# A language-model layer on one core: attention as straight code in place of a loop of four sequences, and the expert lists with one moving operand

## The chip, the cores and the metric

The kernel runs on one core of a Trainium2 chip. The metric is device time in microseconds (us) of one execution; lower is better. The core has TensorE (PE, with PEld its weight loads), VectorE (DVE), ScalarE (ACT), GpSimd (POOL) and SyncE (SP), each with an instruction stream of its own. They meet at semaphores.

## The reference

32 sequences of 512 tokens, width 256, float32:

```
h = (tok_table[x] + pos_table + seg_table[seg]) * sqrt(256)
h = h + attention(layernorm(h))
h = h + ffn(layernorm(h))
attention(x): Q, K, V = x@wq, x@wk, x@wv            # 16 heads of 16, window of 64 keys
              GQ = x@wgq; GK, GV = mean over 8 tokens of x@wgk, x@wgv   # 8 heads, 64 latents
              out = (sigmoid(gl) * local(Q,K,V) + sigmoid(gr) * (remote(GQ,GK,GV) @ r_out_w)) @ w_out
ffn(x): scores = layernorm(x) @ centroids.T          # 8 experts
        expert e takes the 2048 highest scoring tokens that no earlier expert took
        out = x + gelu(layernorm(x) @ w1[e] + b1[e]) @ w2[e] + b2[e], scattered back
```

## The kernel before

The program has two phases. In the **attention** phase the sequences pass through the five engines one by one, software-pipelined: `sequence(b, q)` exists once for each engine and walks through the same `plan` of ten half-steps (scores by query for the row maxima, scores by key, exponentials, values, projections for the next sequence, output of the one before). Every engine computes, at build time, the semaphore count that each of its waits needs, in the class `Misc` (line 409 is one of those waits, issued by PE before it reuses a PSUM bank) and, on VectorE, in `chain` (line 1135), which makes an instruction wait for the one before it.

Sequences 0 and 1 are written out. Sequences 2 to 29 are seven passes through a loop whose body is four sequences, on every engine. Sequences 30 and 31, and step 32, which drains the pipeline, are written out again. On PE:

```
sequence(0, 0)
sequence(1, 1)
with pe.Fori(0, (SEQS - 4) // HB) as i:
    for r in range(HB):
        sequence(HB * i + 2 + r, (2 + r) % HB)
for b in range(SEQS - 2, SEQS + 1):
    sequence(b, b % HB)
```

In the loop `b` is an expression of a register, so each wait whose count depends on `b` is preceded by arithmetic on the engine's sequencer, and addresses of the embedding indices, of the scores and of the stored rows are computed there too. In the written-out sequences they are constants. A sequence of PE begins with `top_scores` for the latents: masks (line 994, 16 matmuls) and then line 1009, 128 small matmuls of 32x64 by 32x64 in one run. Before it stand the waits for what the other engines have to give.

In the **expert** phase (a loop over 7 experts and the eighth written out) PE runs `pe_expert`: per group of 512 tokens the first layer (line 911) and the second (line 924). Between them it serves the choice of the next expert's tokens, `pe_choice` and `dve_choice`, in slots set by the tables `pe_at` and `dve_at`: a radix search for the threshold, then a list of the 2048 chosen tokens. For the list VectorE builds `ohA` (which of 16 columns a token goes to), `ohP` (that times the partition number) and `ohT` (that times 128 x the tile number), and eight pieces `ohB` (lines 1292 to 1302). PE multiplies each `ohB` tile by `ohP` and by `ohT` (line 857), 32 matmuls for a piece, all summed into the 16 columns `LPS`. VectorE copies them into `idx_next` (line 1307), by which GpSimd gathers the rows of the next expert. For expert 0 the same is done before the loop with nothing beside it.

Of the kernel before, what the change touches and what calls it, by code (L numbers as in the profile page):

```python
# [26 lines left out]
P = 128  # L27
# [63 lines left out]
def tower(nc, ins, out, cin, din, widths, SEQS, S, V, F, E):  # L91
# [12 lines left out]
    with ctx:  # L104
# [141 lines left out]

        hits = sb("hits", [P, RADIX - 1, NT], BF16)
        ohA = sb("ohA", [P, NT, CT], BF16)
        ohP = sb("ohP", [P, NT, CT], BF16)
        ohT = sb("ohT", [P, NT, CT], BF16)  # L250
        ohB = sb("ohB", [P, 2, LT, P], BF16)
        w1 = sb("w1", [P, KC, F])
        w2 = sb("w2", [P, FC, D])
# [180 lines left out]
        def _(sp):  # L434
# [43 lines left out]

            store(0, 0)
            store(1, 1)  # L480
            with sp.Fori(0, (SEQS - 4) // HB) as i:
                for r in range(HB):
                    store(HB * i + 2 + r, (2 + r) % HB)
            for b in range(SEQS - 2, SEQS + 1):
                store(b, b % HB)
            sp.wait_ge(s_h1out[0], 16 * (NT // 2 + 1))
            sp.wait_ge(s_h1out[1], 16 * (NT // 2 + 1))
# [99 lines left out]
        def _(pool):  # L587
# [21 lines left out]

            sequence(0, 0)  # L610
            sequence(1, 1)
            with pool.Fori(0, (SEQS - 4) // HB) as i:
                for r in range(HB):
                    sequence(HB * i + 2 + r, (2 + r) % HB)
            for b in range(SEQS - 2, SEQS + 1):
                sequence(b, b % HB)

            pool.wait_ge(s_h1out[0], 16 * (NT // 2 + 1))
# [114 lines left out]
        @block.scalar  # L733
        def _(act):

            act.wait_ge(s_init, 3)
            m = Misc("head")
            for task in head_tasks:
                act_misc(act, m, task, None, 0)

            def sequence(b, q):
                m = Misc(b, q % 2)
                nx = 1 - q % 2
                for s in range(NU):
                    for task in plan[2 * s]:
                        act_misc(act, m, task, b, nx)
                    first, rest = plan[2 * s + 1][0], plan[2 * s + 1][1:]
                    run = m.old if s == 0 else m.new
                    if run:
                        act_exp(act, NU * b + s - 1, (s - 1) % NU, 0)  # L750
                    act_misc(act, m, first, b, nx)
                    if run:
                        act_exp(act, NU * b + s - 1, (s - 1) % NU, 1)
                    for task in rest:
                        act_misc(act, m, task, b, nx)

            sequence(0, 0)
            sequence(1, 1)
            with act.Fori(0, (SEQS - 4) // HB) as i:
                for r in range(HB):  # L760
                    sequence(HB * i + 2 + r, (2 + r) % HB)
            for b in range(SEQS - 2, SEQS + 1):
                sequence(b, b % HB)

            nc.scalar.activation(scr[:, :], c_ident[:, 0:1], ACT.Copy).then_inc(s_hid, 2)
            act_group(act, 0, 0)
            with act.Fori(0, E - 1) as e:
                act_expert(act, e, False)
            act_expert(act, E - 1, True)
# [58 lines left out]
            mm.then_inc(s_misc, 1)  # L828


        LPS = M_ps[1][:, 0:CT]

        def pe_choice(pe, n, part, k):
            if part == "radix":
# [14 lines left out]
            elif part == "list":  # L849
# [2 lines left out]
                    pe.wait_ge(s_ohA, n + 1)  # L852
                pe.wait_ge(s_ohB, LC * n + k + 1)
                for j in range(LT):
                    for half in (ohP, ohT):
                        first_, last_ = k == 0 and j == 0 and half is ohP, k == LC - 1 and j == LT - 1 and half is ohT
                        mm = nc.tensor.matmul(LPS, ohB[:, k % 2, j, :], half[:, k * LT + j, :],
                                              start=first_, stop=last_)
                mm.then_inc(s_used, 1)


# [77 lines left out]
        def _(pe):  # L939
# [169 lines left out]

            sequence(0, 0)  # L1110
            sequence(1, 1)
            with pe.Fori(0, (SEQS - 4) // HB) as i:
                for r in range(HB):
                    sequence(HB * i + 2 + r, (2 + r) % HB)
            for b in range(SEQS - 2, SEQS + 1):
                sequence(b, b % HB)

            pe.wait_ge(s_mA, Misc(SEQS).end("A"))
# [120 lines left out]
        def dve_choice(dve, n, part, k, base):  # L1239
# [51 lines left out]
            elif part == "places":  # L1291
                chain(dve, nc.vector.tensor_tensor(ohA[:, :, :], rhigh[:, :].unsqueeze(2).to_broadcast([P, NT, CT]),
                                                   laneb[:, 0:CT].unsqueeze(1).to_broadcast([P, NT, CT]),
                                                   ALU.is_equal), base)
                nc.vector.tensor_scalar(ohP[:, :, :], ohA[:, :, :], c_part, None, ALU.mult)
                nc.vector.scalar_tensor_tensor(out=ohT[:, :, :], in0=ohA[:, :, :], scalar=float(P),
                                               in1=laneb[:, 0:NT].unsqueeze(2).to_broadcast([P, NT, CT]),
                                               op0=ALU.mult, op1=ALU.mult).then_inc(s_ohA, 1)
            elif part == "list":
# [4 lines left out]
                                        ALU.is_equal).then_inc(s_ohB, 1)  # L1304
            elif part == "numbers":
                dve.wait_ge(s_used, LC * n + LC)
                nc.vector.tensor_copy(idx_next[:, :], LPS).then_inc(s_next, 1)

        def dve_prefix(dve, base):

# [61 lines left out]
        def _(dve):  # L1372
# [96 lines left out]
                    for task in half:  # L1469
                        dve_misc(dve, m, task, b, q, base)  # L1470

            sequence(0, 0, 0)
            PER = CH["n"]
            sequence(1, 1, 0)
            PER = CH["n"] - PER
            base = CH["n"]
            CH["n"] = 0
            with dve.Fori(0, (SEQS - 4) // HB) as i:
                for r in range(HB):
                    sequence(HB * i + 2 + r, (2 + r) % HB, HB * PER * i + base)  # L1480
            assert CH["n"] == HB * PER, CH["n"]
            base += PER * (SEQS - 4)
            CH["n"] = 0
            for b in range(SEQS - 2, SEQS + 1):
                sequence(b, b % HB, base)

            for t in range(TS):
                dve.wait_ge(s_rows[t], 16 * (SEQS + 1))
# [13 lines left out]
            dve_scales(dve, 0, base)  # L1502
            base += CH["n"]
            CH["n"] = 0
            PER2 = 6 * DIGITS + 2 * GR + 23
            with dve.Fori(0, E - 1) as e:
                dve_expert(dve, e, False, PER2 * e + base)
            assert CH["n"] == PER2, CH["n"]
# [32 lines left out]
```

## Time and profile before

| | |
|---|---|
| median of 3 runs | 3180.93 us (3177.55 to 3189.85) |
| the profiled execution's own time | 3194.65 us |
| its span in the trace | 3192.8 us |
| mean granted TensorE clock | 0.945 of full |
| busy: PE, PEld, DVE, ACT, POOL | 2786.0, 1942.8, 1804.9, 1275.4, 873.6 us |
| attention, loop of 28 sequences | 1672.02 us |
| choice for expert 0, with no matrix work beside it | 111.00 us |
| expert phase | 1080.80 us |

PE's busy time and its weight loads overlap. The profiled execution is 13.7 us above the median of the runs. The granted clock of 1 is TensorE's 2.4 GHz, 0.5 is 1.2 GHz. Line numbers (L1009) are those of the code above. "issue" as the end of a wait means that the engine waited for nothing that the profile shows.

### The profile page before, as it was taken

How to read it: one execution, taken by the hardware profiler on the slowest of the kernel's cores; microseconds unless marked ns; L12 is line 12 of the kernel's file. 1: busy time of each engine (PE TensorE's matmuls, PEld its weight loads, DVE VectorE, ACT ScalarE, POOL GpSimd, SP SyncE). 2: the span in 40 equal slices, each digit the busy share in tenths (PEclk: the TensorE clock that was granted, in tenths of full speed). 3: DMA queues.
4: the chain of work that ended last, by engine and by line, in shares of the span. 5: the costliest groups of instructions: out<-in, count | busy, mean ns of one | idle time of the engine just before them, and what ended most of it. 6: DMA issues, size and time to landing. Idle time of an engine off the chain costs nothing. (4 is left out here: it accounts for less than half of the span.)

```text
span 3192.8 us, 118687 instructions
## 1 busy us (share of the span) xinstructions
PE 2786.0 (87%) x49160; PEld 1942.8 (61%) x49160; DVE 1804.9 (57%) x5978; ACT 1275.4 (40%) x2665; POOL 873.6 (27%) x938
## 2 busy tenths in 40 slices
PE   3899989989989989989989998059899999999998
PEld 1566666666666666666666666036565665655666
DVE  3555555555555555555556554667567676665720
ACT  1454444444444444444444442023333333343433
POOL 2212122122122112112112110224353443434443
PEclk9999999999999999999999998569999999999999
DMA  2000000000000000000000000000111101111020
GB/s 62 20 24 22 21 23 24 20 22 21 23 22 20 21 21 24 21 21 24 19 23 24 21 19 15 30 17 31 62 46 49 55 31 63 41 47 61 28 66 27
DMA packets 56398, 98.21 MB, mean 31 GB/s; under 512 B 10332, under 2 KB 41000, under 8 KB 55752
## 3 DMA queue, kind: packets, MB, share of 16 engines
q0 software_dynamic: 18624, 50.88, 5.6%
q1 hardware_dynamic: 37256, 40.07, 3.8%
q8 instruction: 368, 6.03, 0.8%
q14 instruction: 150, 1.23, 0.1%
HBM read 55.78 MB, written 33.55 MB: 28 GB/s over the span
## 5 line engine op out<-in xcount | busy, mean ns | idle before, releaser
L515 POOL DMA_INDIRECT rows<-in_tok_table,idx_now x132 | 138.0, 1045 | 1442.3 <-DVE hres L1154 1368.5
L911 PE MATMUL banks<-hT,w 128*128 128x512 f32 x1024 | 485.0, 622 | 16.1 <-ACT hT L717 12.1
L1176 DVE TENSOR_REDUCE mx<-banks 128x8 f32<-128x1024 f32 x256 | 301.5, 1219 | 204.3 <-PE banks L1014 200.9
L691 ACT ACTIVATE probT<-banks 128x1024 f32<-128x1024 f32 x256 | 262.6, 1026 | 229.8 <-PE banks L1058 229.8
L728 ACT ACTIVATE hid<-banks,b 128x512 f32<-128x512 f32 x256 | 175.2, 687 | 439.1 <-PE banks L911 439.0
L911 PEld LDWEIGHTS banks<-hT,w 128*128 128x128 f32 x1024 | 192.9, 197 | 229.6 <-issue 217.1
L1071 PEld LDWEIGHTS V_ps<-Ve,probT 128*64 128x64 f32 x4096 | 268.9, 147 | 24.9 <-issue 24.9
L1071 PE MATMUL V_ps<-Ve,probT 128*64 128x17 f32 x4096 | 281.8, 217 | 1.4 <-issue 1.4
L1071 PE MATMUL V_ps<-Vo,probT 128*64 128x17 f32 x4096 | 282.0, 217 | 0.2 <-issue 0.2
L1071 PEld LDWEIGHTS V_ps<-Vo,probT 128*64 128x64 f32 x4096 | 268.9, 147 | 0.3 <-issue 0.3
L1251 DVE TENSOR_SCALAR_CACHE_REDUCE hits<-act_s,cval 128x128 bf16<-128x128 f32 x960 | 261.6, 342 | 12.9 <-issue 10.7
L924 PE MATMUL M_ps<-w,hid 128*128 128x256 f32 x1024 | 233.3, 382 | 0.0
L924 PE MATMUL V_ps<-w,hid 128*128 128x256 f32 x1024 | 231.5, 380 | 0.0
L924 PEld LDWEIGHTS V_ps<-w,hid 128*128 128x128 f32 x1024 | 193.1, 190 | 38.4 <-issue 15.3
L924 PEld LDWEIGHTS M_ps<-w,hid 128*128 128x128 f32 x1024 | 191.8, 192 | 23.7
L1197 DVE TENSOR_TENSOR r<-M_ps,sg 128x256 f32<-128x256 f32 x128 | 54.4, 425 | 248.5 <-PE M_ps L799 247.6
L567 POOL TENSOR_TENSOR orow<-orow,b 128x256 f32<-128x256 f32 x128 | 127.1, 993 | 238.1 <-DVE orow L1368 236.7
L1052 PE MATMUL banks<-Qt,Kt 32*64 32x128 f32 x4096 | 184.7, 282 | 0.0
L657 ACT ACTIVATE low<-M_ps 8x256 f32<-8x256 f32 x128 | 47.7, 372 | 326.3 <-PE M_ps L793 326.3
L1052 PEld LDWEIGHTS banks<-Qt,Kt 32*64 32x64 f32 x4096 | 164.1, 132 | 22.7 <-issue 3.8
L571 POOL DMA_INDIRECT out_rows<-orow,idx_cur x128 | 144.4, 1128 | 110.5 <-POOL orow L567 77.3
L1054 PE MATMUL banks<-Qt,Kt 32*64 32x64 f32 x4096 | 173.4, 227 | 0.1
(228 smaller groups left out, 5885.3 us busy)
## 6 DMA issues: line engine op xcount, KB each, us to landing
h_rows<-h SPq DMA_DIRECT2D x128, 128.0 KB, 2.0
w<-in_w SPq DMA_DIRECT2D x16, 1024.0 KB, 5.9
Qt<-low SPq DMA_DIRECT2D x256, 4.0 KB
rows<-in_tok_table,idx_now POOLq DMA_INDIRECT x132, 3.5
out_rows<-orow,idx_cur POOLq DMA_INDIRECT x128, 2.5
cst<-in_tables SPq DMA_DIRECT2D x1, 1060.5 KB
Gq<-lowl SPq DMA_DIRECT2D x64, 8.0 KB
b<-in_b SPq DMA_DIRECT2D x8, 128.0 KB, 5.0
```

What stands on the lines that cost most here:

```text
L515: nc.gpsimd.indirect_dma_start(rows[:, t, :], None, ins["tok_table"], bass.IndirectOffsetOnAxis(idx_now[:, t:t + 1], 0)).then_inc(s_rows[t ...
L567: nc.gpsimd.tensor_tensor(out=orow[:, q % 2, :], in0=orow[:, q % 2, :], in1=b2[:, :], op=ALU.add).then_inc(s_add, 1)
L571: nc.gpsimd.indirect_dma_start(out, bass.IndirectOffsetOnAxis(idx_cur[:, g * GT + q:g * GT + q + 1], 0), orow[:, q % 2, :], None).then_inc ...
L691: nc.scalar.activation(dst[:, 2 * pair:2 * pair + 2, :], banks[:, 2 * pair:2 * pair + 2, :], ACT.Exp).then_inc(s_exp, 1)
L728: nc.scalar.activation(hid[:, m, :], S_ps[m % 2][:, 0:GT * P], ACT.Gelu_apprx_tanh, bias=b1[:, m:m + 1]).then_inc(s_hid, 1)
L911: mm = nc.tensor.matmul(S_ps[m % 2][:, 0:GT * P], w1[:, c, m * P:(m + 1) * P], hT[g % 2][:, c, :], start=c == 0, stop=c == KC - 1)
L924: mm = nc.tensor.matmul(O_ps[q % 2][:, 0:D], hid[:, m, q * P:(q + 1) * P], w2[:, m, :], start=m == 0, stop=m == FC - 1)
L1052: nc.tensor.matmul(banks[side[0], g, n * P:(n + 1) * P], k[:, W + at_:P + at_], q[:, at_:at_ + P], start=False, stop=n == G - 1)
L1054: nc.tensor.matmul(banks[side[1], g, n * P:n * P + W], k[:, at_:W + at_], q[:, at_:at_ + W], start=False, stop=False)
L1071: nc.tensor.matmul(V_ps[side[a], h * OW:(h + 1) * OW], probT[t % 2][:, g, n * P + a * W:n * P + (a + 1) * W], vals[:, t, h, :], start=True ...
L1176: nc.vector.tensor_reduce(tops.rearrange("p (g h) -> p g h", g=2), banks[:, 2 * pair:2 * pair + 2, :].rearrange("p g (h k) -> p g h k", h= ...
L1251: ins_ = nc.vector.tensor_scalar(hits[:, c, :], act_s[:, :], cval[:, c:c + 1].bitcast(F32), None, ALU.is_ge, ALU.add, accum_out=counts[:, ...
```

## The change

All five engines write out sequences 2 to 32 as constants, so that the attention phase has no loop and no register arithmetic. `ohP` and `ohT` become the two halves of one tile `ohN`, 16 columns each, and PE multiplies each `ohB` tile once by both, into 32 columns of PSUM. VectorE copies the first 16 columns to SBUF and adds the other 16 to them. The rest of the attention phase does the same work in the same order.

```diff
-        ohP = sb("ohP", [P, NT, CT], BF16)
-        ohT = sb("ohT", [P, NT, CT], BF16)
+        ohN = sb("ohN", [P, NT, 2, CT], BF16)
@@ sync, gpsimd, scalar and tensor alike (store() on sync)
-            with pe.Fori(0, (SEQS - 4) // HB) as i:
-                for r in range(HB):
-                    sequence(HB * i + 2 + r, (2 + r) % HB)
-            for b in range(SEQS - 2, SEQS + 1):
+            for b in range(2, SEQS + 1):
                 sequence(b, b % HB)
@@ pe_choice
-        LPS = M_ps[1][:, 0:CT]
+        LPS = M_ps[1][:, 0:2 * CT]
...
                 for j in range(LT):
-                    for half in (ohP, ohT):
-                        first_, last_ = k == 0 and j == 0 and half is ohP, k == LC - 1 and j == LT - 1 and half is ohT
-                        mm = nc.tensor.matmul(LPS, ohB[:, k % 2, j, :], half[:, k * LT + j, :],
-                                              start=first_, stop=last_)
+                    mm = nc.tensor.matmul(LPS, ohB[:, k % 2, j, :],
+                                          ohN[:, k * LT + j, :, :].rearrange("p a r -> p (a r)"),
+                                          start=k == 0 and j == 0, stop=k == LC - 1 and j == LT - 1)
@@ dve_choice
-                nc.vector.tensor_scalar(ohP[:, :, :], ohA[:, :, :], c_part, None, ALU.mult)
-                nc.vector.scalar_tensor_tensor(out=ohT[:, :, :], in0=ohA[:, :, :], scalar=float(P),
+                nc.vector.tensor_scalar(ohN[:, :, 0, :], ohA[:, :, :], c_part, None, ALU.mult)
+                nc.vector.scalar_tensor_tensor(out=ohN[:, :, 1, :], in0=ohA[:, :, :], scalar=float(P),
...
-                nc.vector.tensor_copy(idx_next[:, :], LPS).then_inc(s_next, 1)
+                chain(dve, nc.vector.tensor_copy(rank[:, 0:CT], LPS[:, 0:CT]), base)
+                nc.vector.tensor_tensor(idx_next[:, :], rank[:, 0:CT], LPS[:, CT:2 * CT], ALU.add).then_inc(s_next, 1)
@@ vector
-            sequence(0, 0, 0)
-            PER = CH["n"]
...
-            with dve.Fori(0, (SEQS - 4) // HB) as i:
-                for r in range(HB):
-                    sequence(HB * i + 2 + r, (2 + r) % HB, HB * PER * i + base)
...
+            for b in range(SEQS + 1):
+                sequence(b, b % HB, 0)
+            base = 0
```

## Rows read from the trace of the kernel before

**Rows 1.** The page: span, and busy time of each engine

```profile
span 3192.8 us, 118687 instructions
PE 2786.0 (87%) x49160; PEld 1942.8 (61%) x49160; DVE 1804.9 (57%) x5978; ACT 1275.4 (40%) x2665; POOL 873.6 (27%) x938
```

**Rows 2.** Windows by stage: stretch, length, busy (instructions) by engine, clock, DMA

```profile
139.55:194.92 55.37, 52.58 (x1366) 37.95 (x1365) 33.39 (x84) 26.79 (x60) 12.04 (x17) 1.00 0.08 23
194.92:1866.94 1672.02, 1534.25 (x38193) 1108.59 (x38193) 937.51 (x2352) 757.21 (x1653) 337.64 (x449) 0.96 0.08 22
1866.94:1922.80 55.86, 52.37 (x1365) 37.81 (x1364) 26.96 (x62) 26.80 (x60) 0.48 (x1) 1.00 0.05 14
2001.00:2112.00 111.00, 10.49 (x269) 8.66 (x269) 75.27 (x349) 0.00 (x0) 24.85 (x6) 0.50 0.08 25
2112.00:3192.80 1080.80, 1005.26 (x5211) 660.50 (x5211) 641.57 (x2887) 408.27 (x775) 459.46 (x412) 0.97 0.14 46
```

**Rows 3.** Windows, each one sequence of the loop; columns as in rows 2

```profile
194.92:250.93 56.01, 52.66 (x1366) 37.86 (x1366) 33.49 (x84) 27.11 (x60) 11.99 (x17) 1.00 0.09 23
1212.25:1269.49 57.24, 52.67 (x1365) 37.77 (x1364) 33.48 (x84) 27.00 (x60) 11.94 (x17) 1.00 0.08 23
1269.49:1331.29 61.80, 57.18 (x1365) 41.54 (x1364) 33.47 (x84) 27.23 (x60) 12.21 (x17) 0.92 0.08 21
1391.55:1453.50 61.95, 58.19 (x1365) 42.32 (x1365) 32.64 (x82) 25.57 (x52) 11.53 (x16) 0.89 0.08 21
```

**Rows 4.** Waits, whole trace: us in total, times, longest us

```profile
PEld banks L1009 <- issue: 37.9, 33, 1.9
PEld banks L994 <- issue: 31.5, 32, 4.0
```

**Rows 5.** Waits in the window of sequence 30, 1866.94 to 1922.80 us

```profile
PEld banks L1009 <- issue: 1.3, 1, 1.3
```

**Rows 6.** Timeline of PEld, starts of sequence 1 and two others: start, length

```profile
139.79 1.62 PEld L1009 LDWEIGHTS banks<-Gk,Gq 32*64 32x64 f32 x128
...
1269.49 0.16 PEld L994 LDWEIGHTS banks<-cst 32*64 32x64 bf16 x16 [0.33 <-issue]
1269.74 1.34 PEld L1009 LDWEIGHTS banks<-Gk,Gq 32*64 32x64 f32 x100
1272.70 0.34 PEld L1009 LDWEIGHTS banks<-Gk,Gq 32*64 32x64 f32 x28 [1.62 <-issue]
...
1391.55 0.16 PEld L994 LDWEIGHTS banks<-cst 32*64 32x64 bf16 x16 [3.58 <-issue]
```

**Rows 7.** Line 409 alone on PE: ns min/median/max, first and last start

```profile
L409 PEldq ALU_OP  x868: 32/32/42, 196.6 to 1864.2; - x174
```

**Rows 8.** DMA queues during the loop, 194.92 to 1866.94 us: packets, MB, share

```profile
q8 instruction: 313, 5.13, 1.3%
```

**Rows 9.** Windows of one list piece on PE, 2484.00 to 2486.00, line 857 alone

```profile
2484.00:2486.00 2.00, 0.95 (x32) 0.95 (x32) 1.00 0.00 0
```

**Rows 10.** Lines 857, 1295 and 1307, each alone: ns min/median/max

```profile
L857 PE MATMUL M_ps<-ohP,ohB x1024: 168/170/198, 2086.4 to 3049.9; 128*128 128x16 bf16 x171
L1295 DVE TENSOR_SCALAR ohP<-ohA,cst x8: 753/753/754, 2081.1 to 3022.1; 128x2048 bf16<-128x2048 bf16 x8
L1307 DVE CAST idx_next<-M_ps x8: 174/174/175, 2102.8 to 3050.1; 128x16 int32<-128x16 f32 x8
```

**Rows 11.** Timeline of PE in the attention loop: matmuls with 34 columns

```profile
1218.39 0.64 PE L1077 MATMUL V_ps<-bdV,latT 128*64 128x34 f32 x16
```

**Rows 12.** Timeline of VectorE and PEld around the list of the third loop pass

```profile
2496.12 0.42 DVE L1368 TENSOR_TENSOR orow<-M_ps,hrow 128x256 f32<-128x256 f32 x1 [1.33 <-POOLq L579]
2496.46 9.42 DVE L1302 TENSOR_TENSOR ohB<-laneb,rlow 128x2048 bf16<-128x2048 bf16 x4
...
2501.53 0.10 PEld L857 LDWEIGHTS M_ps<-ohP,ohB 128*128 128x128 bf16 x1 [0.78 <-DVE ohB L1302]
2503.73 0.10 PEld L857 LDWEIGHTS M_ps<-ohP,ohB 128*128 128x128 bf16 x1 [0.25 <-DVE ohB L1302]
```

More of the change, by code:

```diff
@@ L480, in _ @@
             store(1, 1)
-            with sp.Fori(0, (SEQS - 4) // HB) as i:
-                for r in range(HB):
-                    store(HB * i + 2 + r, (2 + r) % HB)
-            for b in range(SEQS - 2, SEQS + 1):
+            for b in range(2, SEQS + 1):
                 store(b, b % HB)
@@ L611, in _ @@
             sequence(1, 1)
-            with pool.Fori(0, (SEQS - 4) // HB) as i:
-                for r in range(HB):
-                    sequence(HB * i + 2 + r, (2 + r) % HB)
-            for b in range(SEQS - 2, SEQS + 1):
+            for b in range(2, SEQS + 1):
                 sequence(b, b % HB)
@@ L758, in _ @@
             sequence(1, 1)
[L759 to L762, printed above, removed]
+            for b in range(2, SEQS + 1):
                 sequence(b, b % HB)
@@ L1111, in _ @@
             sequence(1, 1)
-            with pe.Fori(0, (SEQS - 4) // HB) as i:
-                for r in range(HB):
-                    sequence(HB * i + 2 + r, (2 + r) % HB)
-            for b in range(SEQS - 2, SEQS + 1):
+            for b in range(2, SEQS + 1):
                 sequence(b, b % HB)
@@ L1470, in sequence @@
                         dve_misc(dve, m, task, b, q, base)
-            sequence(0, 0, 0)
-            PER = CH["n"]
[L1474 to L1477, printed above, removed]
-            with dve.Fori(0, (SEQS - 4) // HB) as i:
-                for r in range(HB):
-                    sequence(HB * i + 2 + r, (2 + r) % HB, HB * PER * i + base)
[L1481 to L1485, printed above, removed]
+            for b in range(SEQS + 1):
+                sequence(b, b % HB, 0)
+            base = 0
             for t in range(TS):
@@ L1504, in _ @@
             CH["n"] = 0
-            PER2 = 6 * DIGITS + 2 * GR + 23
+            PER2 = 6 * DIGITS + 2 * GR + 24
             with dve.Fori(0, E - 1) as e:
```

## The prediction, made before the changed kernel ran

> **What bounds the kernel now.** I read the page first: PE is busy 2786.0 of 3192.8 us, no other engine above 57% [rows 1]. Then the windows by stage [rows 2]. In the attention loop PE is busy 1534.25 of 1672.02 us (92%) and VectorE 56%; in the expert phase PE 93%. Only the choice for expert 0 (111.00 us) belongs to VectorE. So what the change is worth has to be found on PE: how long one sequence takes there, and what the list pieces hold.
>
> The useful comparison lies inside the trace, for it holds both forms of the code. Sequence 1 is written out and takes 55.37 us between its start on PE and the next one's; sequence 30, also written out, takes 55.86 [rows 2]. Both do the full 1365 matmuls; sequence 30 lacks only the embedding ahead, which is not PE's work (VectorE 26.96 us busy against 33.39). The 28 sequences of the loop take 1672.02 us, 59.7 each. That is 4.1 us a sequence, 115 us in all, between the same work in a loop and as straight code. The windows of single sequences [rows 3] say what it is made of:
>
> - Sequences of the loop at full clock take 56.01 and 57.24 us: mean 56.6.
> - Others are like the one of 61.80 us, with PE's busy time up from 52.7 to 57.2, at a mean granted clock of 0.92. A part of it ran at 1.2 GHz. Over the loop the clock is 0.96 [rows 2], so about 8% of 1672 us, 134 us, at half speed. At half speed a stretch gives up half of itself at most: 67 us.
> - At the loop's back edge PE stands still for 3.58 us before line 994 and nothing releases it ("issue"), where inside the body that gap is 0.33 us [rows 6]. What follows runs at clock 0.89 and takes 61.95 us [rows 3]. All PEld idle time of this kind at line 994 is 31.5 us in 32 waits [rows 4]: 26 of 0.33 us leave some 23 us for six taken back edges, the longest 4.0.
> - In line 1009 PE stops once in most sequences: 37.9 us in 33 waits [rows 4], 1.62 us after 100 of 128 loads in the loop sequence shown, none in sequence 1 [rows 6]. Sequence 30, straight code, has one too, of 1.3 us [rows 5], so the stop is not register arithmetic.
>
> Before the clock falls PE has done little for some microseconds: it waited for the others' results, had the 0.33 us gap, then short matmuls, then the stop of 1.62 us; or the 3.58 us of the back edge. So the clock's loss hangs on these pauses.
>
> Register arithmetic is small on PE: line 409 alone has 868 instructions of 32 ns [rows 7], 31 a sequence, 1 us a sequence if none were covered; most is, as the matmuls already queued run on. 313 instruction fetches of 16 KB fall in the loop [rows 8], 11.2 a sequence. So the loop is fetched anew on every pass and straight code adds no traffic on PE.
>
> **The change, part by part.**
>
> *Back edges go.* Six taken, (3.58 - 0.33) = 3.3 us each on PE's path: -20 us. Ends 20 and 23. The other engines lose theirs too; they have slack.
>
> *Register arithmetic and the moving stop.* The loop at full clock (56.6) against straight code at full clock (mean of 55.37 and 55.86, 55.6): -1.0 us, x28 = -28 us. It holds both the cheaper waits and the stop of line 1009. Where the stop falls depends on where the code is cut into fetched pieces; in the loop that place repeats every four sequences, in straight code it wanders through the whole sequence, so some sequences have a stop and some none. Ends: 56.01 - 55.86 = 0.15 us, -4 us; and 57.24 - 55.37 = 1.87 us, -52 us. I take the middle since I have two samples of each.
>
> *The clock.* Ends: all 67 us stay, or all go. The six starts after a back edge certainly lose their cause; among the others the pause gets shorter or vanishes in part. The two straight windows are both at 1.00 [rows 2]. I take two thirds: -45 us.
>
> *SyncE and GpSimd* run straight code too, and their loops were short. Their streams hold few instructions and GpSimd is busy 12 us in 57 [rows 3]: nothing, covered by waits for the others. Without cover it would be a few stops of at most 3.58 us.
>
> Attention: -20 -28 -45 = -93 us.
>
> *The list on PE.* A piece of 32 matmuls takes 0.95 us [rows 9], one of them 0.17 [rows 10], so one starts every (0.95 - 0.17)/31 = 25 ns. Matmuls with 32 columns are not in the trace in this form. The bounds: 25 ns as with 16 columns; and the nearest row with more columns, 34 in fp32, 16 in 0.64 us, (0.64 - 0.22)/15 = 28 ns [rows 11], 0.22 being one matmul of that kind. I take 25: what sets the pace at 16 columns is not the columns. The piece then costs 0.40 us less (0.36 by the other bound). For 7 experts x 8 pieces, -22 us of PE work; for expert 0 PE waits for VectorE anyway. The Trainium skill (TensorE: Matmul & The Clock Gate, section "Wait — 56ns, not 53.3ns?") puts the floor from start to start near 25 ns however few the columns; the row has 25, and by the page too the 32-column matmul would cost 25, not two of them.
>
> Not all of it reaches the end. VectorE makes the last four `ohB` in one run of 9.42 us, begun only when the row of results before it is free, for which it had waited 1.33 us on GpSimd's queue [rows 12], not on PE. PE already waits for the fifth and the sixth of these pieces (0.78 and 0.25 us of weight-load idle) [rows 12]. So what PE saves in the five pieces before that wait is eaten by it: 5 x 0.40. Three pieces remain: 1.2 us an expert, less 0.1 for a new wait: 1.1 x 7 = -8 us. Ends 0 and 22.
>
> *The list on VectorE.* `ohN`'s halves have 16 elements in a row of 32. Line 1295 now takes 0.753 us for 2048 elements [rows 10], a third of the 2.3 us of line 1302's kind (9.42 us for four [rows 12]). If the gaps cost it that speed, it takes 2.3, +1.5 us an expert ahead of the first piece, +11 us at most. If not, nothing. The inner run is unbroken and a row of 16 is long, so I take nothing. The new copy and the sum cost what line 1307 costs, 0.174 us each, +0.2 us and a chained wait: covered in the loop, since the gather has a group's time; +0.3 us for expert 0, given back by its shorter last piece.
>
> Expert phase: -8 us. **Sum: -101 us**, on the profiled execution 3194.65 - 101 = 3094. That execution was 13.7 us above the median of the runs. I put half of the difference down to slow clock that the other runs had less of, and that can't be won twice: 3180.93 - 101 + 7 = **3087 us**.
>
> **The rivals.**
>
> 1. *The clock keeps falling as often.* The pause at each sequence's start is made of waits that the change doesn't touch, and the stop of line 1009 is found in straight code as well. Then -20 -28 -8 = -56: 3125 us. For it: sequences with and without a back edge fall. Against: both straight windows at 1.00. 17%.
> 2. *Straight code never falls, and the list saving is whole.* -20 -28 -67 -22 = -137: 3044 us. For it: the same two windows. Against: PE's rows with the wait for `ohB`. 13%.
> 3. *Stops for code eat the gain* (the other side). Straight code places the fetch stop anywhere, also where PE's queue is empty. The gain is 101/28 = 3.6 us a sequence; a stop costs 1.6 [rows 6]. From 2.3 additional exposed stops per sequence it is gone; with four, 3180.93 + 28 x (6.4 - 3.6) = 3259 us. For it: 11 fetches a sequence give it room. Against: sequences 1 and 30 issue the same matmuls as straight code and take 55.4 and 55.9. Slower 3%, and 4% that it ends near nothing. The Trainium skill (Runtime: NRT & Kernel Launch, section "Instruction fetch mechanics") says that a taken branch out of the loaded pages forces a fetch, and that in straight code crossing a 16 KiB boundary is mostly hidden. The first agrees with the 3.58 us here. The second would leave no stop in line 1009 and each sequence at 55.4, 7 us less than my sum; the trace's 37.9 us of them speak against it.
>
> **How the numbers follow.** Forecast 63%, rivals 17, 13, 3 and 4%. 3087 is the likeliest. The range reaches to the first two rivals: 3044 to 3130 us, the upper end with 5 us for a slower line 1295. A change of 0.5% (16 us) is about what a measurement of this kernel can tell from none. Faster 0.95, same 0.02, slower 0.03; most of the near-nothing case still saves more than 16 us.
>
> **What would show it.** No gap of over 1 us before line 994. The 28 sequences in about 1580 us, at a mean clock near 0.985. Stops in line 1009 in fewer sequences than now, others elsewhere. Line 409 without arithmetic. 16 matmuls a list piece in 0.55 us. Longer waits at the fifth piece of a list, an expert 134 us instead of 135. Line 1295 still at 0.75 us. The prediction is wrong if the clock stays at 0.96 or if written-out sequences take over 57 us at full clock.

## The result and the profile after

The changed kernel takes **3065.44 us** (median of 4 runs, 3061.5 to 3072.49) against 3185.39 (4 runs) of the kernel before on the same chip: ratio 0.9623, 95% interval 0.9586 to 0.9661, so 3.8% faster. Forecast were 3087 us and a range of 3044 to 3130. The profiled execution took 3072.49 us against 3194.65 of the one before: 122 us less, where the sum of terms said 101.

Line numbers have moved: latent masks 983 (before 994), small matmuls of latent scores 998 (1009), layer 1 900 (911), list 845 (857), `hits` 1237 (1251), `ohB` 1288 (1302).

The page of the changed kernel, span and busy time [before: rows 1]:

```profile
span 3070.7 us, 111586 instructions
PE 2708.5 (88%) x48136; PEld 1876.3 (61%) x48136; DVE 1803.7 (59%) x5986; ACT 1270.0 (41%) x2665; POOL 874.1 (28%) x938
```

Windows of the changed kernel, columns as in [rows 2]: the 28 sequences that were the loop, sequence 30, and (next fence) seven passes of experts:

```profile
193.88:1774.82 1580.94, 1490.66 (x38194) 1072.65 (x38194) 935.55 (x2352) 751.53 (x1653) 338.45 (x449) 0.99 0.08 23
1774.82:1831.70 56.88, 53.93 (x1365) 38.61 (x1364) 26.97 (x62) 27.00 (x60) 0.41 (x1) 0.97 0.04 13
```

```profile
2028.35:2949.02 920.67, 857.66 (x3900) 555.13 (x3900) 622.14 (x2799) 358.11 (x679) 408.83 (x359) 0.99 0.15 47
```

The 28 sequences went from 1672.02 to 1580.94 us: -91.1, forecast -93. The same seven passes of experts (start of the first to start of the last, on line 911) took 950.3 us before: -29.6, forecast -8. The rest (start, last sequences, choice for expert 0) is -1.4. So in this pair of executions the attention part came out as sized and the expert part did not. The clock falls differ from execution to execution: five traces of kernels with the same loop code took 1649.5 to 1681.0 us for the 28 sequences (mean 1665.6), five with the same straight code 1571.6 to 1587.4 (mean 1580.9; table below). On the means the attention part is worth 85 us.

Waits of PEld in the 28 sequences of the changed kernel: us in total, times, longest.

```profile
PEld banks L983 <- issue: 9.6, 29, 0.3
PEld banks L998 <- issue: 7.9, 6, 1.5
...
PEld banks L1047 <- issue: 3.9, 4, 1.4
PEld banks L1043 <- issue: 2.4, 2, 1.7
```

Read it against [rows 4]: line 983 keeps its 0.33 us at every sequence, and none is longer; the back edges are gone. The stop in the small matmuls is left in 6 sequences, 7.9 us in place of 36.5 in the same 28 (37.9 in the whole trace [rows 4]), where 25 sequences had it. A few stops have turned up elsewhere (lines 1043, 1047), as straight code was expected to place them. Instruction traffic hardly moved, as read from [rows 8]; DMA queues in the same window:

```profile
q8 instruction: 302, 4.95, 1.3%
```

Timeline of PEld, starts of sequence 3 and of sequence 26 of the changed kernel:

```profile
249.50 0.16 PEld L983 LDWEIGHTS banks<-cst 32*64 32x64 bf16 x16 [0.33 <-issue]
249.75 1.50 PEld L998 LDWEIGHTS banks<-Gk,Gq 32*64 32x64 f32 x114
252.65 0.23 PEld L998 LDWEIGHTS banks<-Gk,Gq 32*64 32x64 f32 x14 [1.40 <-issue]
...
1552.65 0.16 PEld L983 LDWEIGHTS banks<-cst 32*64 32x64 bf16 x16 [0.33 <-issue]
1552.89 1.62 PEld L998 LDWEIGHTS banks<-Gk,Gq 32*64 32x64 f32 x128
```

Windows of those two sequences: sequence 3 has the stop and a fall of the clock and takes 59.62 us, PE busy 55.85; sequence 26 has neither, 55.05 and 52.54.

```profile
249.50:309.12 59.62, 55.85 (x1365) 40.08 (x1364) 33.39 (x84) 26.90 (x60) 12.08 (x17) 0.94 0.09 22
...
1552.65:1607.70 55.05, 52.54 (x1365) 37.80 (x1364) 33.38 (x84) 26.55 (x59) 12.89 (x18) 1.00 0.09 24
```

The stop and the fall don't always go together. Of the six sequences with the stop, 3 and 24 fell (59.6 and 59.5 us); 8, 14, 19 and 29 stayed at full clock and took 55.9 to 56.3 us. Five more have time at half clock without the stop (5, 22: 6.8 us; 4, 9, 12: 3.4). In the traces of three more kernels with the same PE code here, sequence 3 has the stop and no fall and takes 56.1 to 56.4 us.

**The list in the changed kernel.** Timeline of PE, the eight pieces of the second loop pass [before: rows 9, 12]:

```profile
2247.52 0.56 PE L845 MATMUL M_ps<-ohN,ohB 128*128 128x32 bf16 x16
...
2257.95 0.55 PE L845 MATMUL M_ps<-ohN,ohB 128*128 128x32 bf16 x16
2261.76 0.56 PE L845 MATMUL M_ps<-ohN,ohB 128*128 128x32 bf16 x16 [1.44 <-DVE ohB L1288]
2264.49 0.56 PE L845 MATMUL M_ps<-ohN,ohB 128*128 128x32 bf16 x16 [0.36 <-DVE ohB L1288]
2266.71 0.55 PE L845 MATMUL M_ps<-ohN,ohB 128*128 128x32 bf16 x16
```

A piece takes 0.55 us; one 32-column matmul is 0.176 [next fence], so they start (0.555 - 0.176)/15 = 25 ns apart, as with 16 columns. PE now waits 1.44 and 0.36 us for `ohB`; in the same passes of the kernel before, PE itself had waited for it once (1.2 us), otherwise only the weight loads. Each line alone, ns min/median/max:

```profile
L845 PE MATMUL M_ps<-ohN,ohB x1024: 176/176/209, 1994.1 to 2927.6; 128*128 128x32 bf16 x171
```

```profile
L1281 DVE TENSOR_SCALAR ohN<-ohA,cst x8: 753/754/754, 1988.8 to 2901.0; 128x2048 bf16<-128x2048 bf16 x8
```

```profile
L1293 DVE COPY rank<-M_ps x8: 174/175/176, 2010.1 to 2927.8; 128x16 f32<-128x16 f32 x8
```

Waits of PE in the seven passes of the changed kernel:

```profile
PE M_ps L826 <- DVE hits L1237: 22.8, 14, 2.3
PE M_ps L845 <- DVE ohB L1288: 12.6, 14, 1.4
```

The same passes of the kernel before:

```profile
PE M_ps L836 <- DVE hits L1251: 31.9, 17, 3.1
```

`hits` are the counts for the threshold, VectorE's first long work in a pass, and have nothing to do with the list. Here the unforeseen part of the gain shows, and the experiments start from it.

### The profile page after: what moved, and what is told of

It is laid out like the page before. It is cut to its first block and busy times, and to the rows that moved or that the text cites. A ratio compares the mean times of both kernels' runs of the same rounds, so it can differ in the third digit from the quotient of the medians.

```text
span 3070.7 us, 111586 instructions
## 1 busy us (share of the span) xinstructions
PE 2708.5 (88%) x48136; PEld 1876.3 (61%) x48136; DVE 1803.7 (59%) x5986; ACT 1270.0 (41%) x2665; POOL 874.1 (28%) x938
## 5 line engine op out<-in xcount | busy, mean ns | idle before, releaser
L900 PE MATMUL banks<-hT,w 128*128 128x512 f32 x1024 | 476.1, 611 | 18.5 <-ACT hT L710 12.1
L1060 PE MATMUL V_ps<-Vo,probT 128*64 128x17 f32 x4096 | 270.2, 212 | 3.4 <-issue 3.3
L1060 PE MATMUL V_ps<-Ve,probT 128*64 128x17 f32 x4096 | 270.0, 212 | 3.2 <-issue 2.9
L1060 PEld LDWEIGHTS V_ps<-Ve,probT 128*64 128x64 f32 x4096 | 255.5, 140 | 27.5 <-issue 27.3
L1060 PEld LDWEIGHTS V_ps<-Vo,probT 128*64 128x64 f32 x4096 | 255.6, 140 | 3.8 <-issue 3.8
L913 PEld LDWEIGHTS V_ps<-w,hid 128*128 128x128 f32 x1024 | 192.7, 190 | 38.9 <-issue 15.3
```

Of the source, the lines that this page charges most:

```text
L900: mm = nc.tensor.matmul(S_ps[m % 2][:, 0:GT * P], w1[:, c, m * P:(m + 1) * P], hT[g % 2][:, c, :], start=c == 0, stop=c == KC - 1)
L913: mm = nc.tensor.matmul(O_ps[q % 2][:, 0:D], hid[:, m, q * P:(q + 1) * P], w2[:, m, :], start=m == 0, stop=m == FC - 1)
L1060: nc.tensor.matmul(V_ps[side[a], h * OW:(h + 1) * OW], probT[t % 2][:, g, n * P + a * W:n * P + (a + 1) * W], vals[:, t, h, :], start=True ...
```

## The experiments

Ratios are to the kernel before on the same chip. "28 sequences" and "seven passes" are stretches of the profiled execution as above.

| kernel | median us | ratio, 95% interval | 28 sequences | seven passes | at half clock in the passes |
|---|---|---|---|---|---|
| before | 3185.39 | | 1672.0 | 950.3 | 43.3 |
| before, again | 3197.78 (one run) | | 1681.0 | 945.4 | 33.4 |
| changed | 3065.44 | 0.9623 (0.9586 to 0.9661) | 1580.9 | 920.7 | 18.8 |
| list only | 3177.86 | 0.9988 (0.9959 to 1.0016) | 1654.5 | 932.9 | 28.8 |
| attention only | 3083.17 | 0.9678 (0.9654 to 0.9702) | 1587.4 | 932.8 | 26.6 |
| two loop passes | 3122.93 | 0.9803 (0.9774 to 0.9833) | 1619.7 | 931.3 | 15.5 |
| before, 58 VectorE instructions | 3166.95 | 0.9956 (0.9929 to 0.9982) | 1649.5 | 931.2 | 18.1 |
| changed, 70 VectorE instructions | 3080.79 | 0.9684 (0.9642 to 0.9727) | 1571.6 | 933.0 | 29.1 |
| changed, 128 PE instructions ahead | 3082.2 | 0.9633 (0.9585 to 0.9681) | 1585.9 | 920.3 | 15.2 |
| changed, list pieces later | 3063.13 | 0.9583 (0.954 to 0.9626) | 1578.6 | 908.5 | 15.3 |
| before, list pieces later | 3191.44 | 0.999 (0.9962 to 1.0018) | 1671.0 | 942.4 | 29.5 |
| changed, 24 PE instructions at the start, 49 a sequence | 3407.24 | 1.0626 (1.0522 to 1.0731) | 1890.2 | 920.9 | 18.9 |
| changed, 158 PE instructions at the start, 49 a sequence | 3374.71 | 1.0588 (1.0516 to 1.066) | 1856.8 | 919.1 | 15.2 |

A stage is read from one trace each, so its scatter counts. The same code gave 1649.5 to 1681.0 us (loop) and 1571.6 to 1587.4 us (straight) for the 28 sequences, and 919.1 to 920.9 us for the seven passes of the changed kernel's expert code in four traces. The attention loop's rows therefore can't be compared to a few microseconds; the passes' rows can be read more closely.

**1. The two halves of the change, each alone.** List only: the kernel before with `ohN`, 16 matmuls a piece, and the copy and sum. Its core:

```diff
-                    for half in (ohP, ohT):
-                        mm = nc.tensor.matmul(LPS, ohB[:, k % 2, j, :], half[:, k * LT + j, :],
+                    mm = nc.tensor.matmul(LPS, ohB[:, k % 2, j, :],
+                                          ohN[:, k * LT + j, :, :].rearrange("p a r -> p (a r)"),
```

> The kernel before with the list change alone (ohN, 16 matmuls of 32 columns a piece, the copy and the sum); loops as before. Theory of the prediction: of 22 us of PE work about 8 reach the end, 1.1 to 1.2 us an expert; ratio about 0.997. Rival (the whole expert phase's gain of 29 us comes from the list): ratio 0.991. By the code-placement theory VectorE keeps its stop of 1.6 to 1.9 us inside the first run of line 1251 in every pass of the expert loop, since its code ahead of the loop grows by one instruction only.

Attention only: the changed kernel with the old `ohP`, `ohT` and 32 matmuls a piece put back (the diff above, reversed).

> The changed kernel with the old list (ohP and ohT, 32 matmuls a piece). Theory: attention gives 91 us as in the changed kernel, and the expert phase about 18 us although nothing in it is changed, because VectorE's code ahead of the loop is 58 instructions longer modulo 128 and the loop's code is cut elsewhere; ratio 0.965. Rival (the expert phase's gain belongs to the list): the expert phase stays at 135 us an expert, ratio 0.971.

Measured: attention only keeps 84.6 of the 91.1 us in the 28 sequences (the rest is within their scatter), and it takes 17.5 us off the seven passes, whose code it doesn't touch. List only takes 17.4 us off the passes (2.5 an expert; I had forecast 1.1), but the whole kernel can't be told from the one before: the interval allows a gain of 13 us at most, and the profiled execution was 10 us faster than the median. The wait for `ohB` comes with the short pieces: PE waits 13.2 us for it in list only, and not at all in attention only. So the forecast of "-8 us for the expert phase" missed something that comes with the attention part.

What that is shows on VectorE. In the kernel before it stands still for 1.4 to 1.9 us in `hits`, in six of the seven passes, released by nothing. Timeline of VectorE, second trace of the kernel before:

```profile
2674.93 0.09 DVE L1251 DVE_READ_ACCUMULATOR hits<-act_s,cval 128x1 bf16 x1
2676.93 0.34 DVE L1251 TENSOR_SCALAR_CACHE_REDUCE hits<-act_s,cval 128x128 bf16<-128x128 f32 x1 [1.92 <-issue]
```

Its waits in the seven passes:

```profile
DVE hits L1251 <- issue: 10.4, 6, 1.9
```

The list-only kernel has that row too (9.4 us, 6 times). The changed kernel and the attention-only one have none: in the changed kernel's passes VectorE waits on "issue" only at the back edge.

```profile
DVE b L1328 <- issue: 23.8, 6, 4.3
```

**2. Is it the place of VectorE's code?** Written out, the attention part has another number of VectorE instructions ahead of the expert loop. If code is fetched in pieces of fixed size, the same loop is now cut elsewhere. q14 moved 0.82 MB in 100 packets in the changed kernel, 8.2 KB each, and it is VectorE's queue: an edit on VectorE alone moves its count (150 to 145 with the 58 instructions below, 100 to 106 with the 70), edits on PE alone leave it at 100. I undid that alone, from both sides: 58 empty instructions for the old code, 70 for the new, ahead of the expert phase.

```diff
+            for _ in range(58):      # 70 in the changed kernel
+                stand(dve)           # an empty semaphore increment
```

> The kernel before with 58 empty VectorE instructions (semaphore increments that nobody waits for) where VectorE waits after the attention phase. No work, loop or list is changed. Code-placement theory: the stop of 1.6 to 1.9 us inside the first run of line 1251 leaves every expert pass, an expert takes 132.5 to 133 us instead of 135.3, ratio 0.994 to 0.995. Rival (the gain came from anything else in the change): 135.3 us an expert, ratio 1.000.

> The changed kernel with 70 empty VectorE instructions before the expert phase, which puts the cut of its loop's code back to where it was (58 + 70 = 128). Code-placement theory: the stop inside the first run of the threshold counts returns, an expert takes about 134 us instead of 131.5, 15 to 20 us more than the changed kernel, ratio to before about 0.968. Rival: nothing changes, 0.962.

Measured: with 58 the kernel before loses its stop and the passes go to 931.2 us. With 70 the changed kernel gets it back at the same instructions, and the passes go to 933.0. Timeline and waits of VectorE, the changed kernel with 70:

```profile
2557.16 0.35 DVE L1237 TENSOR_SCALAR_CACHE_REDUCE hits<-act_s,cval 128x128 bf16<-128x128 f32 x1 [1.19 <-issue]
```

```profile
DVE hits L1237 <- issue: 7.6, 6, 1.6
```

The two offsets add up to 128, and the stop is back at the same instruction: 14 of VectorE's recorded instructions lie between the back edge and it, not counting its sequencer's. In the list-only kernel, with one instruction more ahead of the loop, it is 13. The kernel of part 3 has its code moved by 72 instructions; it has no such stop, and its passes take 931.3 us.

So the stop is worth 12 to 16 us: 933.0 - 920.5 with the new list, 948 (mean of two traces) - 932 with the old. The list, with the stop equal on both sides, is worth 11 to 15: 932 - 920.5, or 948 - 933. Part of each is clock. The passes with a stop have 28.8 to 43.3 us at half clock and those without 15.2 to 26.6. Taking off half of that time (the most the clock can have cost), a pass takes 132.7 us in both traces of the kernel before; 131.2 with the new list and the stop (both kernels); 131.4, 131.7 and 131.9 with the old list and no stop; 130.2 and 130.4 with the new list and no stop (130.2 also in the two kernels with 49 empty instructions a sequence, part 4). By this measure the stop is worth 0.7 to 1.3 us a pass, no more than its own length, and the list 1.0 to 1.8; what goes beyond went with the clock.

**3. How much of the gain needs straight code everywhere?** The loop's body is 12 sequences, run twice; sequences 26 to 32 are written out. One back edge is left in place of six; PE's register arithmetic stays in 24 sequences.

```diff
-            with pe.Fori(0, (SEQS - 4) // HB) as i:
-                for r in range(HB):
-                    sequence(HB * i + 2 + r, (2 + r) % HB)
-            for b in range(SEQS - 2, SEQS + 1):
+            with pe.Fori(0, 2) as i:
+                for r in range(12):
+                    sequence(12 * i + 2 + r, (2 + r) % HB)
+            for b in range(SEQS - 6, SEQS + 1):
```

> The kernel before with a loop body of 12 sequences run twice instead of 4 run seven times, sequences 26 to 32 written out: register arithmetic stays in 24 of 28 sequences, five of six back edges go. Theory (pauses and the clock behind them, not the arithmetic): the 28 sequences take 1615 to 1640 us, with full-clock sequences still at 56 to 57 us. Rival (register arithmetic is the cost): 1650 to 1660, only the five edges' own 3.3 us gone. By the code-placement theory the expert phase drops by about 18 us too (its cut moves by 72 instructions).

Measured: 1619.7 us, 52 of the 91 us. The one back edge costs 3.71 us. Stops in line 1009 in 12 of 28 sequences, 75 us at half clock (before 147, changed 38). The full-clock sequences of the loop take 56.6 us, as expected. Five of them, with neither a stop in that line nor a clock fall, take 56.0 us (55.22 to 57.04); seventeen straight ones of the changed kernel, chosen in the same way, take 55.6 (54.80 to 57.18). So register arithmetic costs 0.4 us a sequence at most. Sequence 8 of the kernel before says that even this is too much. It is in the loop, PE's sequencer does 42 arithmetic instructions in it (1.35 us, 31 of them on line 409), it has no stop in line 1009, and it takes 55.2 us, as the eight straight sequences of the changed kernel do that have no stop over 0.5 us beyond one of 0.81 us in line 786 (mean 55.2). The kernel before with 58 VectorE instructions ran the same PE code and did stop there, for 1.63 us. Windows of sequence 8, kernel before and that one:

```profile
547.00:602.18 55.18, 51.96 (x1365) 37.76 (x1365) 33.48 (x84) 26.97 (x60) 12.12 (x17) 1.00 0.09 23
```

```profile
544.02:600.99 56.97, 52.28 (x1365) 37.85 (x1364) 33.47 (x84) 26.96 (x60) 12.09 (x17) 1.00 0.08 23
```

So the stop, not the arithmetic, is what a loop sequence at full clock pays: 1.8 us between these two.

**4. The stop in the small matmuls: is its place that of a cut?** Two attempts. The first fixed the cut in every sequence: 49 empty PE instructions a sequence, with a start that puts the cut inside the small matmuls in all of them, or in none.

```diff
+            for _ in range(158):     # or 24
+                stand(pe)
...
+                    for _ in range(49 if 0 < b < SEQS - 1 else 0):
+                        stand(pe)
                     pe.wait_ge(s_exp, 2 * (NU * b + s - 1))
```

> The same number of empty instructions in each sequence as in the kernel above, but 158 in place of 24 before sequence 0, so that the cut falls about 6 and 262 instructions after the start, in line 998, in every sequence. Theory: a stop of 1.0 to 1.5 us in line 998 in every sequence and a clock that falls in a third to a half of them, 1600 to 1650 us for the 28. Rival (place of the cut without effect): the same time as the kernel above.

> The changed kernel with 49 empty PE instructions in each of sequences 1 to 30, ahead of the wait for the exponentials in the second step, and 24 before sequence 0. Each sequence then has 2816 = 11 x 256 PE instructions, so the code is cut at the same places in each, about 140 instructions after its start. Theory (where the cut falls decides on the stop and on the clock behind it): no stop in line 998 and none over 1 us elsewhere, clock 1.00, 55.0 to 55.5 us a sequence, 1540 to 1555 for the 28 against 1581; ratio to before about 0.953. Rival (the empty instructions cost what they save, or the clock falls whatever the cut): 1580 or more.

With 158, each of the 30 sequences stopped, always at the same load; timeline of PEld, sequence 4:

```profile
344.99 1.50 PEld L1000 LDWEIGHTS banks<-Gk,Gq 32*64 32x64 f32 x114
347.93 0.19 PEld L1000 LDWEIGHTS banks<-Gk,Gq 32*64 32x64 f32 x9 [1.44 <-issue]
```

With 24 none of these 30 did. So the place is right. But as a measure of the stop's cost it failed: both kernels are 6% slower than the one before (ratios 1.0588 and 1.0626). I had taken the empty instructions for covered. They are not. Timeline of PEld, 24 ahead, the line behind the 49:

```profile
367.31 0.23 PEld L990 LDWEIGHTS banks<-cst 32*64 32x64 bf16 x16 [7.04 <-issue]
```

7.04 us for 49 is 0.144 us each, in every sequence; the 158 at the start of the other kernel stand for 22.55 us, 0.143 each. After that pause the clock fell in every sequence of both kernels (6.8 to 23.9 us at half), and in the kernel with 24 the cut landed in line 1049, with a stop of 1.0 to 2.0 us there. The two times say nothing on the stop's price. The traces at hand do: 1.8 us in sequence 8 of the loop (part 3), and in straight code 55.9 to 56.3 us with the stop and no fall against 55.2 without either, about 1 us; with a fall, 59.5 to 59.6.

The second attempt adds no instruction to any sequence, only 128 ahead of PE's first wait, where it stands for 31 us anyway.

```diff
+            for _ in range(128):
+                stand(pe)
             pe.wait_ge(s_load, 16 * LOADS)
```

> The changed kernel with 128 empty PE instructions (semaphore increments) ahead of the first wait for loads, where PE stands for 31 us in any case: 18 us at 0.14 us each, covered. Nothing else is changed, but every piece in which PE's code is fetched (256 instructions) now ends 128 instructions earlier in the kernel's code. In the changed kernel the stop in the small matmuls of line 998 came in sequences 3, 8, 14, 19, 24 and 29 after 115, 109, 128, 123, 117 and 112 loads; a sequence's code is 207 instructions longer than a whole number of such pieces. Theory (the stop is where a piece ends): with the offset the stops must leave these sequences and come in 6, 11, 16 and 21 after about 124, 118, 113 and 107 loads, perhaps in 26 or 27 too; 28 sequences within 8 us of 1581, the kernel's time within 10 us of the changed one's. Rival (the stop belongs to what the sequence does, or comes by chance): the same sequences stop, or others with no such order.

Measured: stops in line 1000 in sequences 6, 11, 16 and 27, at loads 124, 119, 113 and 127; none in 3, 8, 14, 19, 24 or 29. Forecast were 6, 11, 16, 21 at loads 124, 118, 113, 107 and perhaps 26 or 27. (The text put on record says "after" for the number of the load that stopped; the timelines show one fewer before it, 114 for sequence 3 of the changed kernel.) Only 21 misses: there the stop did not show. A fifth stop is in sequence 31, outside the 28. Waits of PEld, whole kernel:

```profile
PEld banks L985 <- issue: 10.7, 32, 0.4
...
PEld banks L1000 <- issue: 7.1, 5, 1.7
```

The rival, that the stop belongs to what the sequence does, falls. In the traces of three more kernels with the PE code of the changed one, sequences 3, 14, 19 and 24 stop at the same loads every time (115, 128, 123 and 117); 8 and 29 do so in two of the three. So a place is fixed by the code, but a stop there need not show in each execution. The 28 sequences took 1585.9 us against 1580.9, which is within their scatter: a shift of all cuts moves single sequences by up to 6 us, and no change of the sum is shown.

**5. What holds the list's saving back?** My step said that what PE saves in five of eight pieces is eaten by its wait for VectorE's run of four `ohB`. If so, the pieces have only to come later. No instruction is added.

```diff
-                 (3, 0): [("list", 3)], (3, 1): [("list", 4)], (3, 2): [("list", 5)], (3, 3): [("list", 6)],
+                 (3, 0): [("list", 3)], (3, 2): [("list", 4)], (3, 3): [("list", 5)], (3, 4): [("list", 6)],
```

> The changed kernel with PE's list pieces 4, 5 and 6 one slot later, behind the layer-1 matmuls of m = 2, 3 and 4 of the last group instead of m = 1, 2 and 3; the same instructions in all, none added. In the changed kernel PE waits 1.4 us for the fifth piece's ohB and 0.4 us for the sixth's, in each of six experts. Theory (what the list's shorter pieces save is held back by VectorE's run of four ohB, and nothing else follows from it): one slot is 1.7 us, so the first wait goes whole and the second as well; 1.3 to 1.8 us an expert come back, passes of the loop go from 131.5 to about 130 us, and the kernel is 8 to 11 us faster than the changed one. Rival (the wait is for the end of VectorE's whole run, and piece 7, which stays where it is, takes it over): passes stay at 131.5 us and a new wait of 1 to 2 us stands ahead of the last piece.

> The same shift of list pieces 4, 5 and 6 in the kernel before, which has pieces of 0.95 us and waits of its own for ohB of 0.1 to 0.5 us in each expert. Theory: it gains less than the changed kernel does from the same shift, under 0.5 us an expert, 0 to 3 us in all, as there is next to no wait to take back. Rival (a slot later is of use whatever the pieces' length, as the order of the stage is what counts): a gain like the changed kernel's, 8 us or more.

Measured in the changed kernel: seven passes 908.5 us, 12.2 less than the changed kernel's and 1.7 an expert. Window and PE's wait for `ohB` (12.6 us before the move):

```profile
2030.92:2939.39 908.47, 854.92 (x3900) 554.59 (x3900) 622.34 (x2799) 358.07 (x679) 408.87 (x359) 0.99 0.15 48
```

```profile
PE M_ps L845 <- DVE ohB L1288: 1.8, 7, 0.3
```

The wait was real and nothing took its place. In the old code the same move gave 942.4 us, 7.9 less than the first trace of before, where I had expected at most 3. So I took a second trace of the kernel before.

> The kernel before once more, for a second trace of it. In its first trace seven passes of the expert loop took 950.3 us with 43.3 us at half clock; less half of that, 132.7 us a pass. The same kernel with three list pieces moved took 942.4 us with 29.5 us at half clock: 132.5 a pass less half of that. Theory (the move of the pieces is worth nothing in the old code, and the 7.9 us between the two are falls of the clock, which differ from execution to execution): passes of 132.4 to 132.9 us less half the half-clock time, whatever their sum, VectorE's stop in line 1251 in six passes, and 28 sequences of the attention loop in 1660 to 1685 us. Rival (the move is worth 1 us an expert): 135.5 us or more a pass at a half-clock time near 29 us.

```profile
2128.90:3074.30 945.40, 885.19 (x4795) 580.78 (x4795) 620.61 (x2792) 358.28 (x679) 409.90 (x359) 0.98 0.14 46
```

945.4 us with 33.4 at half clock. Less half of the half-clock time, a pass is 132.67 us in both traces of before and 132.52 with the move; for the new list 130.18 and 128.69. The move is worth 1.5 us an expert with the new list. With the old it is 0.15, which can't be told from nothing (three traces of one expert code lay between 131.4 and 131.9). That is as the theory says.

The changed kernel with the later pieces is the fastest version: ratio 0.9583 against 0.9623. The intervals overlap and the two ran on different chips, so the whole time doesn't settle it; the stage does, with -12 us where four traces without the move lay within 1.8 us.

## Why the prediction was right, and where it was not

- *Back edges, -20.* Right. The six gaps of the profiled execution were 3.58 to 4.05 us, 20.8 beyond the 0.33 that stays; none is left.
- *Register arithmetic and moving stop, -28.* Right, -31. Full-clock sequences went from 56.83 (10 of the loop, without the ones that hold a back edge) to 55.73 (21 straight ones): 1.1 us x 28. Five traces of each code give 56.94 and 55.89, nearly the same. The runs split it as I couldn't: the rarer stop is nearly all of it, the arithmetic 0 to 0.4 us. The cover that I suspected ("most is") was there: 1.35 us of arithmetic in sequence 8, none of it in its 55.2 us.
- *The clock, -45 (ends 0 and 67).* The remainder of the stage over its full-clock sequences and back edges went from 59.9 to 20.5 us: -39. It was the least supported term (two thirds of an upper end, with no row to divide it), and that it landed near its value is partly luck: half of the half-clock time that went away is 54.6 us in this pair of traces, and 31 to 77 by which trace of the loop is set against which of the straight code. Two rows of windows at clock 1.00 had spoken for all of it; the clock still fell in 8 of the sequences 1 to 30, so rival 2 was too bold there. My reason, that the falls hang on these pauses, is borne out only in the sum: fewer pauses, fewer falls. Single stops in straight code mostly passed without a fall (21 of 27 in five traces). Rival 1 (the clock falls as often, 3125 us) is out: 147 us at half clock became 38 (102 to 171 in five traces of the loop, 17 to 41 in five of straight code).
- *SyncE and GpSimd, nothing.* No run speaks against it, though none tried it alone: the undisturbed straight sequences take 55.2 us, less than either straight one of before [rows 2].
- *The list on PE, 0.40 us a piece.* Exact: 0.55 us and 25 ns from start to start. The Trainium skill (TensorE: Matmul & The Clock Gate, section "Wait — 56ns, not 53.3ns?") has that floor for narrow moving operands, and the trace agrees with 25 ns at 32 columns.
- *Only 1.1 us an expert of it reaches the end.* The mechanism was right: wait at the fifth piece and its removal by the later slots are both shown. The size was low. With the stop equal on both sides it is 1.6 to 2.1 us an expert, and 1.0 to 1.8 less the clock's share. Part of what was missing went with fewer falls of the clock; that the shorter pieces caused this isn't shown.
- *VectorE's line 1295 stays at 0.75, copy and sum covered.* Right, 0.754 and 0.175 us.
- **The step that failed: "Expert phase: -8 us".** It counted only the list. The term that is missing is VectorE's stop of 1.4 to 1.9 us in `hits` at the start of each expert pass, which went away because the code ahead of the loop got another length. It is worth 12 to 16 us of the 29.6 (24.7 against the second trace of before). It stood in the trace of before and I had not looked at VectorE's waits in that stage. On PE I applied just this thought (the cut wanders when the code ahead changes), and on VectorE not.
- *Rival 3, stops for code eat the gain.* Straight code does have stops in new places (lines 1043, 1047, 1060), of 0.7 to 1.7 us, but in some ten of 28 sequences, not the 2.3 more per sequence that would have cost the gain. The Trainium skill (Runtime: NRT & Kernel Launch, section "Instruction fetch mechanics") says that an engine's code comes in blocks of 256 instructions and that crossing into the next is mostly hidden. The first agrees with where PE's stops went under an offset of 128, but not with VectorE: its queue's packets have 8.2 KB where PE's (q8) have 16.4, and offsets of 58 and 70 together brought its stop back to the same instruction, both of which fit pieces of 128 instructions; there the measurement decides. The second holds for most of the 11 fetches a sequence and not for those in the short matmuls, where the runs show 0.5 to 2.1 us.

What stays open: whether the expert pass's clock falls are caused by the stop in each case or only go with it (28.8 to 43.3 us at half clock with it, 15.2 to 26.6 without; nothing was tried on the clock alone), what makes the clock fall behind one stop and not behind another, and what in sequence 21 hid the stop that the offset should have put there, as a stop at one and the same place shows in some executions and not in others.

## What to carry to other kernels

An edit that changes how much code stands ahead of a loop moves the places at which the loop's own code is cut, on each engine by itself; look for "issue" gaps that recur at the same instruction in every pass, on every engine that others wait for, and count them among the terms. When one part of a stage gets faster on one engine, ask in the same edit which slot now waits for its partner: moving three pieces by one slot was worth as much as the list's edit itself. Compare stages less half of their half-clock time as well as whole: it turned two traces that differed by 5 us into the same 132.67 us a pass. But find out how far traces of the same code lie apart before reading a difference; here it was up to 0.6 us a pass and 31 us in the attention loop. And before a loop's register arithmetic is blamed for its time, look for one pass of it without any stop.

## What the runs showed of the hardware

- An empty semaphore increment on PE's stream costs 0.144 us when 49 stand in a row ahead of a matmul (7.04 us), and 0.143 us when 158 do (22.55 us); it isn't hidden by matmuls already queued.
- PE's code stops at places that can be computed: with an offset of 128 instructions four of five came where forecast, within one load. Inside runs of short matmuls a stop is 0.5 to 2.1 us; most other fetches show no gap.
- Register arithmetic on PE's sequencer, 42 instructions and 1.35 us in a sequence of 55 us, can be covered whole: sequence 8 of the loop takes 55.2 us like undisturbed straight code.
- VectorE has the same kind of stop, 1.1 to 1.9 us, 13 or 14 of its recorded instructions behind a taken back edge, if a cut lies there; 58 or 70 empty instructions ahead of the loop remove it or bring it back.
